# Running the FFN matmuls of one column chunk under the quantization of the next, and moving the residual add into the output projection

## The reference

```python
xn = _layernorm(x, axis=-1)
x = x + _L0_attn_ref(xn, Wq, Wkv, Wk, Wv, Wo, q_g, k_g) + _L0_ffn_ref(xn, weight, bias)
```

## Time and profile before

| | us |
|---|---|
| median of 2 runs | 5611.3 |
| the two runs | 5582.4 and 5640.2 |
| the profiled execution, its own time | 5583.3 |
| span of its slowest core (core 1) | 5581.8 |
| spans of all eight cores | 5556.3 to 5581.8 |

### The profile page before, as it was taken

How to read it: one execution, slowest core, us unless ns; L and a number is a source line. 1 busy time by engine, 2 the same in 40 slices (tenths; PEclk the granted TensorE clock), 3 DMA queues, 4 the chain that set the end, 5 groups by cost and what they waited for, 6 DMA issues and landing times.

```text
span 5581.8 us, 62494 instructions; the slowest of 8 cores (5556.3 to 5581.8 us)
## 1 busy us (share of the span) xinstructions
PE 3164.7 (57%) x25970; PEld 2311.4 (41%) x25970; DVE 1500.5 (27%) x2629; ACT 603.7 (11%) x589; POOL 85.2 (2%) x164
## 2 busy tenths in 40 slices
PE   0555277766201151524277777777777677767388
PEld 0333155555100020201126666653666546636388
DVE  7222411111677736464520000001000010010311
ACT  0000000000000000000002333320333213303000
POOL 0000000000000000000000000000000000000022
PEclk6555577777555575757578777776877768768599
DMA  4111300000000000000000000000000000000022
GB/s 123 45 34 38 102 16 12 12 16 8 15 14 12 4 27 4 27 4 26 6 13 1 1 1 1 1 1 1 1 1 1 1 1 1 1 15 3 15 58 65
DMA packets 50861, 102.02 MB, mean 18 GB/s; under 512 B 8534, under 2 KB 26774, under 8 KB 50584
## 3 DMA queue, kind: packets, MB, share of 16 engines
q1 hardware_dynamic: 45464, 89.50, 5.0%
q0 software_dynamic: 5120, 8.53, 0.6%
HBM read 81.09 MB, written 16.78 MB: 18 GB/s over the span
## 4 chain that ended last, share of the span: by engine, by line
PE 55%; DVE 25%; issue 11%; ACT 6%; DMA 1%; DVEq 1%; SPq 0%; POOL 0%; ACTq 0%; POOLq 0%
PE psA L146 33%; PE psB L146 16%; PE psA L151 6%; ACT arena L817 6%; DVE arena L350 3%; DVE arena L348 2%; DVE arena L480 1%; DVE arena L375 1%; DVE arena L373 1%; DVEq L103 1%; DVE arena L378 1%; DVE arena L642 1%; DVE arena L654 1%; DVE arena L542 1%; DVE arena L344 1%
## 5 line engine op out<-in xcount | busy, mean ns | idle before, releaser
L146 PE MATMUL psA<-arena 32*128 32x128 f32 (+5 forms) x15936 | 1831.5, 339 | 278.7 <-DVE arena L889 102.2
L146 PEld LDWEIGHTS psA<-arena 32*128 32x128 f32 (+3 forms) x15936 | 1372.9, 222 | 765.1 <-issue 732.1
L146 PE MATMUL psB<-arena 128*64 128x128 f32 (+3 forms) x9234 | 1018.8, 368 | 739.4 <-ACT arena L817 503.8
L146 PEld LDWEIGHTS psB<-arena 128*64 128x64 f32 (+3 forms) x9234 | 809.5, 188 | 897.5 <-issue 883.9
L151 PE MATMUL psA<-arena 128*128 128x128 f32 (+1 forms) x736 | 324.1, 440 | 1353.4 <-DVE arena L363 835.4
L151 PEld LDWEIGHTS psA<-arena 128*128 128x128 f32 (+1 forms) x736 | 131.1, 178 | 1545.5 <-issue 1545.5
L817 ACT ACTIVATE arena<-psA,arena 128x1024 f32<-128x1024 f32 x544 | 580.0, 1111 | 1587.6 <-PE psA L146 1587.6
L849 DVE TENSOR_TENSOR arena<-psB,arena 128x1024 f32<-128x1024 f32 x24 | 29.4, 1225 | 1046.5 <-PE psB L146 1046.5
L845 DVE COPY arena<-psB 128x1024 f32<-128x1024 f32 x16 | 19.6, 1225 | 778.5 <-PE psB L146 778.5
L350 DVE TENSOR_TENSOR arena<-arena 128x1024 f32<-128x1024 f32 x144 | 176.4, 1225 | 15.0
L728 ACT ACTIVATE arena<-psA,arena 16x1024 f32<-16x1024 f32 x4 | 4.4, 1107 | 1558.4 <-PE psA L146 1558.4
(11 more groups left out here) (76 smaller groups left out, 943.7 us busy)
## 6 DMA issues: line engine op xcount, KB each, us to landing
arena<-xb SPq DMA_DIRECT2D x64, 512.0 KB, 3.4
arena<-xown SPq DMA_DIRECT2D x48, 512.0 KB, 3.4
out<-arena SPq DMA_DIRECT2D x32, 256.0 KB, 2.0
arena<-out POOLq DMA_DIRECT2D x128, 64.0 KB, 2.5
out<-arena SPq DMA_DIRECT2D x128, 64.0 KB, 2.2
arena<-wq SPq DMA_DIRECT2D x8, 512.0 KB, 9.4
arena<-fw SPq DMA_DIRECT2D x8, 512.0 KB, 3.3
arena<-wop SPq DMA_DIRECT2D x8, 512.0 KB, 6.1
```

Source lines behind the costliest of these rows:

```text
L146: lambda e: e.matmul(out, lhsT, rhs, start=start, stop=stop, tile_position=tp, skip_group_check=skipg),
```

## The change

In stage C, tokens, the matmuls of chunk oc - 1 are now issued in the program's loop turn oc, in two halves of four blocks: `ffn_half(oc - 1, 0..3)`, two tiles of chunk oc, the DVE copies and stores of the half (`tf_half`), `ffn_half(oc - 1, 4..7)`, two more tiles, and again `tf_half`. The loop has a fifth turn without tiles. `xdfm` becomes a double buffer `xdfm2`, its second half where `xfm` was; the matmuls use banks 4 to 7, the transposes banks 0 and 1. The second eight transposes and copies of a tile (L654) are gone; the add L676 becomes a plain copy from PSUM, so that `out` holds only the FFN part. In stage E the residual is added by PE: a slot loads its 512 KB of x into `xet` (the two buffers that were `probs`) on SP's queue, and each of the eight output blocks of the slot gets a ninth matmul with that tile against the identity.

```diff
+            def ffn_half(oc_p, jlist):
+                po = oc_p % 2
+                cw_p = min(512, OWN - 512 * oc_p)
+                for j in jlist:
+                    bk = 4 + j % 4
+                    for ci in range(8):
+                        mm(bank(bk, 0, cw_p),
+                           wdT(ci)[:, 128 * j:128 * j + 128],
+                           xdfm2(po, ci, 0, cw_p), ci == 0, False,
+                           waits=([t_sub_oc[oc_p], t_wdT] if ci == 0
+                                  else []) +
+                                 ([t_prev_f[j % 4]] if ci == 0 and
+                                  t_prev_f[j % 4] else []), inc=False)
+                    bias_mm[(oc_p, j)] = mm(
+                        bank(bk, 0, cw_p), fbr(128 * j, 128), onesr(cw_p),
+                        False, True, waits=[t_or])
+
+            def tf_half(oc_p, jlist):
+                cw_p = min(512, OWN - 512 * oc_p)
+                for j in jlist:
+                    bk = 4 + j % 4
+                    hb = 512 * (j % 2)
+                    t_f = dve(lambda e, j=j, bk=bk, hb=hb, cw_p=cw_p:
+                              e.tensor_copy(scr2(hb, cw_p), bank(bk, 0, cw_p)),
+                              waits=[bias_mm[(oc_p, j)]] +
+                                    ([t_pw[-2]] if len(t_pw) >= 2 else []))
+                    t_prev_f[j % 4] = t_f
+                    t_pw.append(dma("sync", dout[...], scr2(hb, cw_p), waits=[t_f]))
...
+            for oc in range(n_oc + 1):
+                subs = (list(range(min(512, OWN - 512 * oc) // 128))
+                        if oc < n_oc else [])
+                hh = (len(subs) + 1) // 2
+                par = oc % 2
+                if oc >= 1:
+                    ffn_half(oc - 1, [0, 1, 2, 3])
+                for sub in subs[:hh]:
+                    if qtile(4 * oc + sub, par):
+                        return
+                if oc >= 1:
+                    tf_half(oc - 1, [0, 1, 2, 3])
+                    ffn_half(oc - 1, [4, 5, 6, 7])
+                for sub in subs[hh:]:
+                    if qtile(4 * oc + sub, par):
+                        return
+                if oc < n_oc:
+                    t_sub_oc[oc] = hold["t_sub"]
...
+                if oc >= 1:
+                    tf_half(oc - 1, [4, 5, 6, 7])
...
-                    for ci in range(8):
-                        tp = pet(bank(2 + ci // 4, 128 * (ci % 4), 128),
-                                 tmt(bi)[:, 128 * ci:128 * ci + 128], idt(),
-                                 waits=[t_l, w.tok("dv")])
-                        t_sub = dve(lambda e, ci=ci, sub=sub: e.tensor_copy(
-                            xfm(ci, 128 * sub, 128),
-                            bank(2 + ci // 4, 128 * (ci % 4), 128)), waits=[tp])
...
+            t_xuse = [None, None]
             for s in range(nslot):
+                sb = s % 2
+                t_xl = dma("sync", xet(sb)[:], dxo[128 * s:128 * s + 128, :],
+                           waits=[t_pe_end] +
+                                 ([t_xuse[sb]] if t_xuse[sb] else []))
                 for jg in range(2):
                     for j in range(4 * jg, 4 * jg + 4):
                         bk, off = 2 + j // 4, 128 * (j % 4)
                         for u in range(8):
...
+                        t_c = mm(bank(bk, off, 128),
+                                 xet(sb)[:, 128 * j:128 * j + 128], idt(),
+                                 False, j % 4 == 3, waits=[t_xl],
+                                 inc=j % 4 == 3)
```

More of the change, by code:

```diff
@@ L263, in build_nc @@
         wdT = lambda i: tl(o_R4 + i * 1024, 1024)
-        xfm = lambda j, off=0, w=512: tl(o_R4 + 8192 + j * 512 + off, w)
+        xdfm2 = lambda p, i, off=0, w=512: tl(
+            (o_R6 if p == 0 else o_R4 + 8192) + i * 512 + off, w)
+        xet = lambda i: tl(o_probs + 1024 * i, 1024)
         accslot = lambda s, off=0, w=1024: tl(o_R4 + s * 1024 + off, w)
@@ L623, in emit @@
             t_prev_f = [None] * 4
[L624 to L635, removed]
+            n_oc = (OWN + 511) // 512
@@ new lines, in emit @@
+            t_sub_oc = [None] * n_oc
+            bias_mm = {}
+            def ffn_half(oc_p, jlist):
[14 more added lines that the diff above has]
+                        False, True, waits=[t_or])
@@ new lines, in tf_half @@
+            def tf_half(oc_p, jlist):
[8 more added lines that the diff above has]
+                    t_prev_f[j % 4] = t_f
+                    t_pw.append(dma("sync",
+                                    dout[128 * j:128 * j + 128,
+                                         512 * oc_p:512 * oc_p + cw_p],
+                                    scr2(hb, cw_p), waits=[t_f]))
@@ new lines, in emit, with qtile @@
+            hold = {"t_sub": None}
+            def qtile(ot, par):
+                bi = ot % 2
+                t_l = dma("sync", tmt(bi)[:], dxo[128 * ot:128 * ot + 128, :],
+                          waits=[tuse[bi]])
+                t_qz = quant(w, o_tm + bi * 1024,
+                             None if stop_after == 'Cq2' else stc(2, ot),
+                             None if stop_after == 'Cq2' else stc(3, ot),
+                             [t_l])
+                if stop_after in ("Cq", "Cq2") and ot == 0:
+                    dma("sync", dout[0:128, 0:min(OWN, 1024)],
+                        qtm()[:, 0:min(OWN, 1024)], waits=[t_qz])
+                    w.waitall_sync()
+                    return True
+                sub = ot % 4
+                t_sub = hold["t_sub"]
+                for ci in range(8):
+                    tp = pet(bank(ci // 4, 128 * (ci % 4), 128),
+                             qtm()[:, 128 * ci:128 * ci + 128], idt(),
+                             waits=[t_qz, w.tok("dv")])
+                    t_sub = dve(lambda e, ci=ci, sub=sub, par=par:
+                                e.tensor_copy(
+                        xdfm2(par, ci, 128 * sub, 128),
+                        bank(ci // 4, 128 * (ci % 4), 128)), waits=[tp])
+                if stop_after == "Cx" and ot == 0:
+                    dma("sync", dout[0:128, 0:min(OWN, 512)],
+                        xdfm2(0, 0, 0, min(OWN, 512)), waits=[w.tok("dv")])
+                    w.waitall_sync()
+                    return True
+                tuse[bi] = t_qz
+                hold["t_sub"] = t_sub
+                return False
@@ new lines, in emit @@
+            for oc in range(n_oc + 1):
[16 more added lines that the diff above has]
+                    t_sub_oc[oc] = hold["t_sub"]
+                    if stop_after == "C1" and oc == 0:
+                        cw1 = min(OWN, 512)
+                        for ci in range(8):
+                            dma("sync", dout[128 * ci:128 * ci + 128, 0:cw1],
+                                xdfm2(0, ci, 0, cw1), waits=[w.tok("dv")])
@@ L636, in emit @@
                         w.waitall_sync()
                         return
-                    for ci in range(8):
-                        tp = pet(bank(ci // 4, 128 * (ci % 4), 128),
-                                 qtm()[:, 128 * ci:128 * ci + 128], idt(),
-                                 waits=[t_qz, w.tok("dv")])
-                        t_sub = dve(lambda e, ci=ci, sub=sub: e.tensor_copy(
-                            xdfm(ci, 128 * sub, 128),
-                            bank(ci // 4, 128 * (ci % 4), 128)), waits=[tp])
@@ L657, in emit @@
[L657 to L683, removed]
@@ L931, in emit @@
                         for u in range(8):
[L932 to L939, removed]
+                            mm(bank(bk, off, 128),
+                               wo_u(u)[:, 128 * j:128 * j + 128],
+                               accslot(s, 128 * u, 128),
+                               u == 0 and j % 4 == 0, False,
+                               waits=[t_nm_s[s], wo_tok[u], w.tok("dv")],
+                               inc=False)
+                        t_c = mm(bank(bk, off, 128),
+                                 xet(sb)[:, 128 * j:128 * j + 128], idt(),
+                                 False, j % 4 == 3, waits=[t_xl],
+                                 inc=j % 4 == 3)
                     wo_close[jg] = t_c
+                t_xuse[sb] = wo_close[1]
                 for j in range(8):
```

## The result

The changed kernel takes 5457.5 us (median of 11 runs, 5410.5 to 5486.3) where the kernel before takes 5625.5 (median of 10). The ratio is 0.973, 95% interval 0.967 to 0.979: faster by 2.7%, where 3.3% and a time of 5346 to 5455 us were forecast. The direction held; the time is 2.5 us above the top of the range. The executions of either kernel fall into two groups (5575 to 5589 and 5614 to 5691 us before, 5410 to 5414 and 5450 to 5486 after), and every ratio here leaves out those in which one half of the chip's cores ran markedly slower than the other, which is why it is not the quotient of the medians.

A forecast was written before the change was run, and what follows sets the result against it. PE and DVE were taken to alternate in stage C, its chunks costing the sum of both, with PE the bound in the projection. 5583.3 - 295 (stage C) + 110 (stage E) = 5398 us; range 5346 to 5455.

The forecast's parts named there:

- Steps 1 to 5: Stage C: transpose pairs removed, matmuls hidden beside quantization, less copies, load waits and last matmuls; 1078.4 to 783.7 us, gain 295.
- rival of unhidden halves: Stage C: beside a working DVE the FFN matmuls stay at the low clock; +125 us, total 5523; 8%.
- Step 6: Stage E, output projection: eight more matmuls per slot, 1.82 us each slot.
- Step 7: Stage E: PE stalls for the load of x behind the last slot's stores; 3.5 us (2.8 to 5.4) in 15 slots.
- Step 8: Stage E: PE's clock drops at the gap in each slot, and its rise costs 1.9 us per slot.
- small E: Rival, stage E: load lands in 3.4 us and the clock stays up; +71 us, total 5359; 16%.
- lost clock: Rival, stage E: the clock falls at the stall and stays low within the slot; +330 us, total 5618; 4%.
- large E: Rival, stage E: the load of x takes 6.1 us to land; +139 us, total 5427; 14%.

The follow-up runs named there:

- e_prefetched: The changed kernel with each projection slot's load of x issued one slot ahead, before the stores of the slot; 5381.2 us, ratio 0.953 to the kernel before.
- e_quiet: The changed kernel without POOL's loads of the FFN part in the projection, but for the first eight; 5453.7 us in its one execution.
- e_filled: The changed kernel with 17 filling matmuls before the first that needs x, in slots 1 to 15; 5422.8 us, ratio 0.968.
- e_only: The kernel before with only stage E of the change, so x is added twice; two runs, 5761 and 5815 us.
- best: The changed kernel with the projection's x load one slot ahead and stage C tile loads issued earlier; 5295.6 us, ratio 0.9465 to the kernel before.

## Why the prediction was wrong, point by point

**Steps 1 to 5, stage C: right.** 783.7 us forecast, 784.7 on core 1 between the same instructions; a gain of 294 to 295 us for 295. Its parts were measured apart: 125 us for the pairs (127), 168 for the overlap. The half shown ended 8.3 us before its cover did (8 forecast), a `tf_half` cost 4.3 us, and the five loads 26.0 us for 28.0. The rival of unhidden halves did not come: the first copies of a tile wait 0.70 us for PE, at most 1.05, as before.

**Step 6, the extra matmuls: right.** 28.5 us for 29 (e_prefetched).

**Step 7, the load: mis-sized by 0.7 us per slot.** 3.5 us forecast, 4.1 to 4.3 on cores 4 to 7, inside its bounds (2.8 to 5.4). The term that failed is the landing, taken as 4.1 us from a load behind one store, in fact the first of two loads issued together; it is 4.5 to 4.7 in the projection, and e_quiet shows POOL's four loads to be 0.9 of it. The load also goes out 0.15 us later than counted. The page DMA: Bandwidth & Descriptors of the Trainium skill (Latency and other measured facts), named in the forecast for its fixed cost growing under load, agrees in direction: 3.7 without POOL's loads, 4.6 with them. No run here separates a fixed cost from the sharing of the transfer itself, and the 6.0 us that the forecast set beside that page is of two loads in flight at once.

**Step 8, the clock: right in kind and, where no 0.81 occurred, in size.** What is left of core 5's 125.2 us after 29.1 for matmuls and 64.2 for the wait is 31.9, 2.1 per slot; core 4 gives 122.0 - 29.1 - 62.7 = 30.2, 2.0. Forecast 1.9. Of this, 0.2 is not the clock: the first eight matmuls, cut off from the others, take 2.02 us in the trace and not 1.82. The rest, 27.0 us on core 4 and 28.9 on core 5, is by how much the 64 matmuls behind the waits exceed 14.53 us. That PE's idle time in the stall causes it is shown by e_filled. It is not as sure in each slot as the forecast has it: on cores 4 to 7 the clock falls at 57 of the 60 waits. Core 4 has one of the three others:

```profile
5170.34 14.53 PE L146 MATMUL psA<-arena 128*128 128x128 f32 x128 [3.61 <-DMA arena<-xown]
```

The length of the wait does not decide it: the clock stayed up at waits of 3.57 to 3.83 us and fell at one of 3.54.

**The total: the step that failed.** On cores 4 to 7 the spans are 5395 to 5406 us against the 5398 forecast, in part by luck: their projections grew by 119 to 125 us and not 110, and an attention 4 to 12 us shorter than core 1's in the profile before offset it. The slowest core is core 1, and its execution is the median one, so the 59.5 us between 5398 and 5457.5 can be laid out on it:

- 29.0 us are attention, a term that the forecast put at nothing because the change touches nothing in it ("Attention should take its 2316 us again"). All of it lies behind 4399 us, where the clock of 0.81 begins.
- 22.2 us are step 8: 139.5 - 29.1 - 59.7 = 50.7 us, 3.4 per slot, where 28.5 were forecast. The clock falls at each of the 15 waits. In the eight slots without 0.81 the 64 matmuls behind the wait lose 15.0 us in sum, 1.9 each as forecast; in the seven that have 0.81 in them they lose 30.3, or 4.3 each.
- 7.2 us are step 7: 59.7 us of waiting where 52.5 were forecast.
- The rest, 1 us, is spread over the other stages.

So the forecast knew two values of the clock, 0.5 and 1.00, and the 0.81 between them was in none of its terms: on cores 4 to 7, which had no 0.81, its sum comes out to within 8 us. It also took the scale of one profiled execution and put 15 us into the range for what no change touches. The two runs then shown, 5582 and 5640, already lay 58 us apart. With that spread in the range, 5346 to some 5500 us, the time would have lain inside. The four lowest executions of each kernel have medians of 5582.5 and 5411.5 us: a gain of 171, against the 185 forecast.

In the ten profiles no core without stretches at 0.81 in its attention takes more than 2329 us for it. They come in pairs of cores (0 and 1, 2 and 3, 4 and 5, 6 and 7), beginning within 15 us of each other. That all of core 1's 29 us are theirs rests on where they lie; no experiment switched them off. e_only has them without the new stage C, and best has none with it. What brings them on, and on which pair, was not tried and stays open. Nothing shows that the changed kernel meets them more often: 4 of its 11 executions lie below 5420 us, and 11 of the 24 of the kernel before below 5600.

**The other rivals.** The small E (+71) and the lost clock (+330) did not come; the large E (+139) is what core 1 showed, but by the clock and not by a landing of 6.1 us.

## What to carry to other kernels

Two engines that take turns in a stage cost the sum of their times, and a program order that puts one's work of step n - 1 beside the other's of step n gets back most of it (168 of 203 us here), if the work fits in the cover: compare both durations before. When a term is moved elsewhere, follow its DMA through its queue: here the residual should have cost 8 matmuls per slot where it went, and cost four times that, because its load stood behind stores that wait for the end of the slot before; issued one slot earlier the load was free here. A stall in a burst of matmuls costs its own length and then, nearly every time here, the clock behind it. And before a range is drawn, look at how far apart whole executions lie, and why: what no change touches still moved by 29 us.

## What the runs showed of the hardware

- The granted clock has a value between the two usual ones. Stretches of some 20 us at 0.81 (core 0, above, with PE busy for 16.1 of 20 us) come on some cores in some profiles, always on both cores of a pair, and the same matmuls take longer there: 64 of them behind a wait 18.61 us on core 1, 17.09 on core 4. The Trainium skill describes this in TensorE: Matmul & The Clock Gate, the peak-current limiter: a die goes to 13/16 of the clock, 1.95 GHz, once three of its cores run dense matmuls. 0.81 is that figure. It does not hold at all times, though: cores 4 to 7 ran the same dense bursts at 1.00 in the profile after, and all eight did in the profile before. Nor did the whole die have it: cores 2 and 3 had 1.00 in attention and projection of the profile after, where cores 0 and 1 had 0.81.
- Waits of 3.5 to 5.1 us between two bursts cost 1.5 to 1.9 us more per slot in the matmuls behind them on cores 4 to 7, at 57 of 60 waits, and nothing once 17 idle matmuls filled them (0.91 to 1.00 in mean clock). In e_quiet waits of 2.8 to 3.3 us mostly did the same.
- A load of 512 KB took 3.4 us from issue to landing at the median of the kernel before, 3.7 beside the projection's stores of 64 KB, and 4.6 with POOL's loads of 64 KB as well. Its place in the queue cost more than its landing: 93 to 97 us of the projection, and 28 us of stage C.
